# Transpositions alternate with the matmuls of the products on TensorE, and four engines get a new order of calls

## The chip, the cores and the metric

The kernel runs on one core of a Trainium2 chip. The metric is the time of the whole kernel on the device, in microseconds, as the median of the runs: 535.18 us before the change, over 3 runs (534.74 to 535.26).

A core has five engines that run side by side, each with its own list of instructions that it works through in order: TensorE (PE, matmuls and transpositions, results in PSUM), VectorE (DVE), ScalarE (ACT), GpSimd (POOL) and SyncE (SP, which only starts DMAs here). They meet only at semaphores.

## The reference

One decoder layer over x of shape (4, 1024, 256), with a context of (4, 77, 256). Cut to what is computed:

```python
# 1. self-attention with sigmoid weights, keys and queries normalised
q, k, v = x @ Wq.T + bq, x @ Wk.T + bk, x @ Wv.T + bv
attn = sigmoid(layer_norm(q) @ layer_norm(k).T / sqrt(256) - log(1024))
x = layernorm(x + ((attn @ v) @ Wo.T + bo) * layerscale)
# 2. cross-attention over 77 context rows, 16 heads of 16
a = softmax(qh @ kh.T / 4)
x = layernorm(x + (a @ vh) @ dense_w.T + dense_b)
# 3. feed-forward with a shift by one row
x_prev = x shifted down by one row
r = sigmoid((mu_r * x + (1 - mu_r) * x_prev) @ W_r.T)
k = (mu_k * x + (1 - mu_k) * x_prev) @ W_k.T
x = layernorm(x + r * (square(relu(k)) @ W_v.T))
```

## The kernel before

The 4096 rows of x are cut into 32 row tiles of 128 rows, t = 0 to 31, and 16 pairs of tiles (256 rows), i = 0 to 15, four pairs to a batch. The score work of self-attention is cut further, into 64 blocks, four to a pair.

**Products in three parts.** A product of two fp32 matrices is done as hi times hi, hi times lo and lo times hi, where hi is the operand rounded to fp32r and lo the rest. So every product is a run of 12 matmuls of 256 columns (6 of 512 columns for `qk`), all issued by `split_product` at line 298. ACT makes the hi part (line 477), DVE or POOL the lo part (line 1299, lines 971 and 990).

**Calls.** Each engine's program is a list of calls of small functions, one for each step and tile. On TensorE these are:
- products: `qk(t)` (queries and keys), `v(i)`, `scores(n)` and `attend(n)` (self-attention, n = 0 to 63), `query(i)` and `dense(i)` (cross-attention), `receptance(i)`, `mix_keys(i)`, `mix_values(i)` (feed-forward);
- transpositions of 128x128 fp32 blocks with the identity in `columns`: `tqk(t)` (line 1973, 4 turns), `x1(i)` and `x2(i)` (line 1885, 4 turns each), and `weights_t(t, c)` (line 2077), which turns the softmax weights of tile t in three groups c = 0, 1, 2 of 4, 4 and 2 turns. In all 576 turns;
- small fp32 matmuls: `cross_scores(t)` (line 2064, 32 rows at a time) and `mixed(i)` (line 2096, 32 columns at a time).

**Self-attention.** `scores(n)` fills one of two PSUM banks, ACT takes the sigmoid (`sigmoid`, line 553) and rounds it (`sigmoid_hi`), DVE makes the rest (`sigmoid_lo`), `attend(n)` multiplies with v and adds over the four blocks of a pair.

**Cross-attention of a tile.** `cross_scores(t)` fills four banks. DVE takes the largest of each head (`maxima(t, g)`, g = 0 to 3, line 1412), ACT takes 16 exponentials (`exponentials(t, g)`, four in a group, line 594), POOL adds halves (`fold_weights`, line 1047), DVE finishes sums and reciprocals, POOL multiplies (`normalise`, line 1052). Then `weights_t(t, c)` turns the weights into the first two of those banks, DVE copies them out (lines 1432 and 1438, ACT some), and `mixed(i)` and `dense(i)` follow for the pair. ACT has to load another table (line 545, helper `table_for`) whenever it changes between sigmoid and exponential.

Two waits matter below. `weights_t(t, 0)` writes into a bank of `cross_scores(t + 1)`, which has been issued before it, so it waits for the first group of that tile's exponentials; its second group of turns waits for the second:

```python
w.wait_ge(*pn_pool.at(t))            # normalise(t)
...
elif t + 1 < NT:
    w.wait_ge(*ex_act.at(t + 1, c + 1))
```

And `dense(i)` waits for the third group of exponentials of tile 2i+3, whose bank it writes.

**The order.** Each engine's list is written out by hand for the start and the end. Between them stand rounds: a function `round_(r)` holds the calls of one pair's worth of work on that engine, every stage some pairs behind the stage ahead of it, and `at(...)` leaves out the calls whose tile isn't there yet. The last 60 us or so are feed-forward work, with rounds `mix_round(i)` that place a few calls. No scheduler stands behind it: what is written is what the engine runs, in that order.

## Time and profile before

| | |
|---|---|
| median of the runs | 535.18 us (534.74 to 535.26) |
| span of the profiled execution | 531.8 us |
| PE busy | 515.0 us, 97% |
| PE weight loads | 468.3 us, 88% |
| ACT busy | 450.4 us, 85% |
| DVE busy | 443.7 us, 83% |
| POOL busy | 381.9 us, 72% |
| ACT table loads | 58, 74.4 us |

The span runs from the first to the last instruction of the one execution that the profiler recorded. It is 3.4 us shorter than the median of the timed runs, which have what lies around the instructions in them; the profile does not give the profiled execution's whole time apart. Sums are made against the span, and their difference is added to the median.

How to read it: a PE record of a matmul reaches from its start to a modelled end, and the next one starts long before that, so "busy" does not say that TensorE runs at its peak. What a matmul costs is the distance from its start to the start of the next one. Where rows stand in order of time, the first column is the start and the second the duration; `x4` is four instructions merged into a row.

### The profile page before, as it was taken

To read this page: it belongs to the slowest core of one execution; us is meant where nothing else is said; L and a number is where in the kernel's file an instruction comes from. 1 tells how busy PE (TensorE), PEld (TensorE's weight loads), DVE (VectorE), ACT (ScalarE), POOL (GpSimd) and SP (SyncE) were. 2 spreads that over 40 slices of the span, in tenths; PEclk is the share of its full clock that TensorE was granted. 3 is DMA by queue.
4 is the path that set the end of the run, shared out by engine and by line. 5 is a ranking of instruction groups with operands and counts; after the bars stand their busy time and mean duration, and the time that the engine had idled before them with its cause. 6 is when DMAs were issued, how large, how long until landed. Compare 5 with 4: busy or idle time off the path is not lost.

```text
span 531.8 us, 12709 instructions
## 1 busy us (share of the span) xinstructions
PE 515.0 (97%) x4530; PEld 468.3 (88%) x4530; DVE 443.7 (83%) x995; ACT 450.4 (85%) x1130; POOL 381.9 (72%) x554
## 2 busy tenths in 40 slices
PE   9999999999999999999999999999999898999994
PEld 6888999898989898989898989999898787899994
DVE  4787868878888879797979797778878888999996
ACT  3765579998989898989898989899999899898965
POOL 1774747676867676767667675767778889897996
PEclk9999999999999999999999999999999999999998
DMA  6410120110010110101010100020511000011122
GB/s 193 128 49 21 38 60 6 42 39 2 14 50 27 35 38 24 42 19 52 12 39 3 39 2 22 21 74 28 166 35 41 2 2 1 22 41 41 41 80 100
DMA packets 23269, 22.50 MB, mean 42 GB/s; under 512 B 1724, under 2 KB 23204, under 8 KB 23205
## 3 DMA queue, kind: packets, MB, share of 16 engines
q1 hardware_dynamic: 22770, 21.35, 12.7%
q8 instruction: 36, 0.59, 0.5%
q10 hardware_dynamic: 434, 0.34, 0.2%
q14 instruction: 29, 0.23, 0.2%
HBM read 14.55 MB, written 6.82 MB: 40 GB/s over the span
## 4 chain that ended last, share of the span: by engine, by line
PE 70%; ACT 12%; DVE 9%; issue 4%; POOL 4%; POOLq 0%; DVEq 0%; ACTq 0%
PE st L298 16%; PE acc L298 14%; PE xb L298 10%; PE proj L298 10%; PE xb L2077 5%; PE xb L2096 5%; ACT p_sb L594 4%; PE xb L2064 4%; DVE xm L1485 3%; ACT L545 2%; PE proj L1973 2%; PE xb L1885 1%; POOL rs L1110 1%; PE st L1893 1%; DVE kkT_lo L1299 1%
## 5 line engine op out<-in xcount | busy, mean ns | idle before, releaser
L594 ACT ACTIVATE p_sb<-xb,neg_mx 128x77 f32<-128x77 f32 x512 | 120.0, 366 | 5.2 <-DVE neg_mx L1412 4.9
L1047 POOL TENSOR_TENSOR fold<-p_sb 128x640 f32<-128x640 f32 x32 | 50.2, 1568 | 75.4 <-ACT p_sb L594 75.1
L1052 POOL TENSOR_TENSOR p_sb<-p_sb,rc 128x1280 f32<-128x1280 f32 x32 | 75.3, 2353 | 23.8 <-DVE rc L1425 23.7
L298 PE MATMUL acc<-vv_hi,aT_hi 128*128 128x256 f32 x256 | 76.6, 299 | 0.0
L545 ACT ACT_TABLE_LOAD x58 | 74.4, 1283 | 1.0
L298 PE MATMUL st<-qkT_hi 128*128 128x256 f32 x256 | 74.8, 292 | 0.0
L298 PE MATMUL st<-qkT_lo,qkT_hi 128*128 128x256 f32 x256 | 72.4, 283 | 0.0
L298 PE MATMUL st<-qkT_hi,qkT_lo 128*128 128x256 f32 x256 | 72.4, 283 | 0.0
L298 PE MATMUL acc<-vv_lo,aT_hi 128*128 128x256 f32 x256 | 72.2, 282 | 0.0
L298 PE MATMUL acc<-vv_hi,aT_lo 128*128 128x256 f32 x256 | 72.2, 282 | 0.0
L1412 DVE TENSOR_REDUCE neg_mx<-xb 128x4 f32<-128x308 f32 x128 | 53.7, 467 | 17.1 <-PE xb L2064 16.7
L553 ACT ACTIVATE a_sb<-st,nlogs 128x512 f32<-128x512 f32 x64 | 43.3, 679 | 16.4 <-PE st L298 16.3
L298 PEld LDWEIGHTS st<-qkT_hi 128*128 128x128 f32 x256 | 48.9, 191 | 4.9 <-issue 4.1
L1299 DVE TENSOR_TENSOR aT_lo<-a_sb,aT_hi 128x512 fp32r<-128x512 f32 x64 | 49.0, 767 | 4.1 <-ACT aT_hi L477 3.2
L298 PEld LDWEIGHTS acc<-vv_hi,aT_hi 128*128 128x128 f32 x256 | 48.6, 190 | 3.4 <-issue 3.3
L1432 DVE COPY pT<-xb 128x512 f32<-128x512 f32 x64 | 43.1, 676 | 10.1 <-PE xb L2077 9.8
L2077 PE MATMUL xb<-columns,p_sb 128*128 128x128 f32 x320 | 48.4, 274 | 1.7 <-DVE pT L1432 0.6
L298 PEld LDWEIGHTS st<-qkT_lo,qkT_hi 128*128 128x128 f32 x256 | 49.0, 191 | 0.2
L298 PEld LDWEIGHTS st<-qkT_hi,qkT_lo 128*128 128x128 f32 x256 | 48.9, 191 | 0.0
L298 PEld LDWEIGHTS acc<-vv_lo,aT_hi 128*128 128x128 f32 x256 | 48.8, 191 | 0.1
L298 PEld LDWEIGHTS acc<-vv_hi,aT_lo 128*128 128x128 f32 x256 | 48.7, 190 | 0.0
L477 ACT ACTIVATE aT_hi<-a_sb 128x512 fp32r<-128x512 f32 x64 | 43.2, 679 | 2.8 <-PE acc L298 2.6
(262 smaller groups left out, 1707.9 us busy)
## 6 DMA issues: line engine op xcount, KB each, us to landing
xs<-in_x SPq DMA_DIRECT2D x16, 256.0 KB, 3.0
xraw<-in_xT SPq DMA_DIRECT2D x15, 256.0 KB, 2.9
out_y<-y SPq DMA_DIRECT2D x15, 256.0 KB, 2.1
x_kept<-xs SPq DMA_DIRECT2D x10, 256.0 KB, 2.2
x2s_a<-x_kept SPq DMA_DIRECT2D x2, 512.0 KB, 5.0
x2s_b<-x_kept SPq DMA_DIRECT2D x2, 512.0 KB, 7.1
x2s_c<-x_kept SPq DMA_DIRECT2D x1, 512.0 KB, 3.7
cT<-in_cT SPq DMA_DIRECT2D x1, 308.0 KB, 3.3
```

What stands on the lines that cost most here:

```text
L298: mm = pe.matmul(out, s_, m_, start=first and k == 0 and q == 0, stop=last and k == n - 1 and q == 2, skip_group_check=not check)
L477: return act.activation(out, in_, ACT.Identity, **kw)
L545: act.activation(spare[:, n:n + 1], nlogs[:], func)
L553: act.activation(a_sb[:, i % NAR], st_bank[i % 2], ACT.Sigmoid, bias=nlogs[:, 0:1], scale=1.0 / 16).then_inc(sg_act.sem, 1)
L594: ex = act.activation(weights(t)[:, h // KH * (H // 2) + KH * n + h % KH, 0:SC], logits[n][:, h * SC:(h + 1) * SC], ACT.Exp, bias=neg_mx[: ...
L1047: pool.tensor_tensor(fold[:].rearrange("p (h k) -> p h k", k=FO), p[:, :, 0:FO], p[:, :, FO:2 * FO], ALU.add).then_inc(fo_pool.sem, 1)
L1052: pool.tensor_tensor(weights(t), weights(t), rc[:, t % 2].rearrange("p (h o) -> p h o", o=1) .to_broadcast([P, H, SP]), ALU.mult).then_inc ...
L1299: return dve.tensor_tensor(lo, whole, f(hi), ALU.subtract)
L1412: dve.tensor_reduce(neg_mx[:, t % 2, HG * n:HG * (n + 1)], logits[n][:, 0:HG * SC].rearrange("p (h k) -> p h k", k=SC), AX, ALU.min)\
L1432: dve.tensor_copy(pT[:, 4 * c:4 * c + 4, (t % 2) * P:(t % 2 + 1) * P], tiles(tp_bank(c), 4))\
L2077: mm = pe.transpose(tp_bank(c)[:, (n - 4 * c) * P:(n - 4 * c + 1) * P], p_sb[:, t % NP, n * P:(n + 1) * P], ident)
L2096: mm = pe.matmul(mixed_bank(i)[32 * n:32 * (n + 1), k * D:(k + 1) * D], vb[:, n, half, :, :, KC * b + k].rearrange("p a d -> p (a d)"), pT ...
```

## The change

On TensorE the four functions of transpositions (`tqk`, `x1`, `x2`, `weights_t`) become generators that give up control after each turn. `split_product` takes such a generator as `beside` and pulls one turn from it after each of its matmuls. `woven(product, i, turns...)` issues a product with turns between its matmuls, and what is left of the turns behind it; `alone(turns)` issues turns by themselves. The semaphore of a product or of a group of turns is still counted up by its own last matmul. About 550 of the 576 turns now stand between two matmuls of products; `weights_t(22, 2)`, `x2(0)`, `weights_t(31, ...)`, `x2(5)` and `x2(6)` stand alone.

```diff
+        NONE = iter(())
+
-        def split_product(pe, out, stationary, moving, first=True, last=True, check=True):
+        def split_product(pe, out, stationary, moving, first=True, last=True, check=True, then=None, beside=NONE):
             n = len(stationary)
             for k in range(n):
                 (sh, sl), (mh, ml) = stationary[k], moving[k]
                 for q, (s_, m_) in enumerate(((sh, mh), (sh, ml), (sl, mh))):
                     mm = pe.matmul(out, s_, m_, start=first and k == 0 and q == 0,
                                    stop=last and k == n - 1 and q == 2, skip_group_check=not check)
-            return mm
+                    if then and k == n - 1 and q == 2:
+                        mm.then_inc(then, 1)
+                    next(beside, None)
...
+        def alone(turns):
+            for _ in turns:
+                pass
+
+        def woven(call, i, *turns):
+            beside = chain(*turns)
+            call(i, beside)
+            alone(beside)
```

The second part is a new order of the calls on TensorE, ACT, DVE and POOL; the set of calls, the functions' waits, the buffers and the numbers that split work between engines stay as they are, and each engine issues as many instructions of each kind as before. The new round of TensorE is below whole. It runs for r = 7 to 12; what comes before and behind is written out.

```diff
                 def round_(r):
-                    at(attend, 4 * r - 18, NS, 9)
...
+                    attend(4 * r - 17)
+                    woven(qk, 2 * r, weights_t(2 * r - 13, 2))
+                    mixed(r - 7)
+                    scores(4 * r - 13)
+                    cross_scores(2 * r - 11)
+                    v(r)
+                    attend(4 * r - 16)
+                    attend(4 * r - 15)
+                    woven(dense, r - 7, weights_t(2 * r - 12, 0), tqk(2 * r))
+                    woven(scores, 4 * r - 12, x1(r - 5))
+                    qk(2 * r + 1)
+                    woven(query, r - 5, weights_t(2 * r - 12, 1), weights_t(2 * r - 12, 2))
+                    scores(4 * r - 11)
+                    cross_scores(2 * r - 10)
+                    scores(4 * r - 10)
+                    woven(attend, 4 * r - 14, weights_t(2 * r - 11, 0), tqk(2 * r + 1), weights_t(2 * r - 11, 1))
```

At the start, `on_all_rows(0)` and `on_all_rows(1)` (biases spread over all rows, line 1899) move ahead of `first_qk`, and `wvo()` comes before `qk(4)`:

```diff
                 warm_up()
+                on_all_rows(0)
+                on_all_rows(1)
                 first_qk()
-                on_all_rows(0)
                 qk(2)
                 qk(3)
-                on_all_rows(1)
-                qk(4)
-                tqk(0)
                 wvo()
+                woven(qk, 4, tqk(0))
```

In the written-out end of TensorE's list, `receptance(0)` to `receptance(2)` and `mix_keys(2)` move ahead of `cross_scores(31)`, `mixed(14)` is followed at once by `dense(14)`, and the three groups of `weights_t(31, ...)` stand in a row.

What stands in a row on TensorE in a round, before: the end of `dense`, and behind it the turns of the softmax weights, of queries and keys and of x, then the first matmul of `attend`.

```order
L298 MATMUL xb<-wx_lo,oT_hi 128x256
L298 MATMUL xb<-wx_hi,oT_lo 128x256
L2077 MATMUL xb<-columns,p_sb 128x128 [waits s_pn_pool]
L2077 MATMUL xb<-columns,p_sb 128x128 x3
L1973 MATMUL proj<-columns,qk_sb 128x128 [waits s_v_dve,s_qn_dve]
L1973 MATMUL proj<-columns,qk_sb 128x128 x3
L1885 MATMUL xb<-columns,xs 128x128 [waits s_ex_act,s_ln1_act]
L1885 MATMUL xb<-columns,xs 128x128 x3
L298 MATMUL acc<-vv_hi,aT_hi 128x256 [waits s_ln1a_dve,s_st_dve]
```

The same place after: the whole of `dense` with the turns of the weights and of queries and keys between its matmuls (the matmuls of products are at line 301 now, the turns at 2392 and 2286).

```order
L301 MATMUL xb<-wx_hi,oT_hi 128x256 [waits s_ex_act]
L2392 MATMUL xb<-columns,p_sb 128x128 [waits s_pn_pool]
L301 MATMUL xb<-wx_lo,oT_hi 128x256
L2392 MATMUL xb<-columns,p_sb 128x128
L301 MATMUL xb<-wx_hi,oT_lo 128x256
L2392 MATMUL xb<-columns,p_sb 128x128
L301 MATMUL xb<-wx_hi,oT_hi 128x256
L2392 MATMUL xb<-columns,p_sb 128x128
L301 MATMUL xb<-wx_lo,oT_hi 128x256
L2286 MATMUL proj<-columns,qk_sb 128x128 [waits s_v_dve,s_qn_dve]
L301 MATMUL xb<-wx_hi,oT_lo 128x256
L2286 MATMUL proj<-columns,qk_sb 128x128
```

The run of 12 turns is gone; each turn has a matmul of a product on either side.

The second place is the stretch behind `cross_scores` of an even tile, TensorE, before: `cross_scores`, then `attend` and `scores` (24 matmuls, of which the first and the last stand here), then the turns that wait for the exponentials of that tile.

```order
L2064 MATMUL xb<-kb,xq 128x154 x7
L298 MATMUL acc<-vv_hi,aT_hi 128x256 [waits s_st_dve]
...
L298 MATMUL st<-qkT_hi,qkT_lo 128x256
L2077 MATMUL xb<-columns,p_sb 128x128 [waits s_ex_act,s_pn_pool]
L2077 MATMUL xb<-columns,p_sb 128x128 x3
```

After:

```order
L2378 MATMUL xb<-kb,xq 128x154 x7
L301 MATMUL st<-qkT_hi 128x256 [waits s_sg_act]
...
L301 MATMUL st<-qkT_hi,qkT_lo 128x256
L301 MATMUL acc<-vv_hi,aT_hi 128x256 [waits s_v_pool,s_st_dve]
L2392 MATMUL xb<-columns,p_sb 128x128 [waits s_ex_act,s_pn_pool]
L301 MATMUL acc<-vv_lo,aT_hi 128x256
```

Between `cross_scores` and the first turn that waits for its exponentials there stand 13 matmuls now, where there were 24.

## Rows read from the trace of the kernel before

**Rows 1.** The page: busy time, share of the span and instructions of each engine.

```profile
PE 515.0 (97%) x4530; PEld 468.3 (88%) x4530; DVE 443.7 (83%) x995; ACT 450.4 (85%) x1130; POOL 381.9 (72%) x554
```

**Rows 2.** Busy by stretch: start:end, length; engines with counts, PEclk, DMA share, GB/s.

```profile
90.00:181.00 91.00, 90.88 (x829) 83.22 (x832) 77.39 (x168) 84.07 (x217) 60.89 (x77) 1.00 0.10 31
181.00:337.00 156.00, 156.00 (x1460) 143.39 (x1455) 132.84 (x295) 141.97 (x371) 106.89 (x146) 1.00 0.09 27
...
401.00:465.00 64.00, 58.50 (x569) 51.37 (x562) 56.51 (x134) 55.82 (x157) 57.02 (x71) 1.00 0.04 14
465.00:525.00 60.00, 58.17 (x473) 56.39 (x471) 57.11 (x141) 51.06 (x107) 54.54 (x101) 1.00 0.15 50
```

**Rows 3.** PE in order of time around groups of twelve and of two turns.

```profile
202.13 0.28 PE L298 MATMUL st<-qkT_hi,qkT_lo 128*128 128x256 f32 x1
202.25 0.60 PE L2077 MATMUL xb<-columns,p_sb 128*128 128x128 f32 x4
202.68 0.60 PE L1973 MATMUL proj<-columns,qk_sb 128*128 128x128 f32 x4
203.12 0.60 PE L2077 MATMUL xb<-columns,p_sb 128*128 128x128 f32 x4
...
203.68 0.28 PE L298 MATMUL acc<-vv_lo,aT_hi 128*128 128x256 f32 x1
...
204.87 0.28 PE L298 MATMUL acc<-vv_hi,aT_lo 128*128 128x256 f32 x1
204.99 0.38 PE L2077 MATMUL xb<-columns,p_sb 128*128 128x128 f32 x2
...
205.44 0.40 PE L298 MATMUL proj<-wqk_lo,xT_hi 128*128 128x512 f32 x1
205.68 0.39 PE L298 MATMUL proj<-wqk_hi,xT_lo 128*128 128x512 f32 x1
```

**Rows 4.** Weight loads (PEld) in order of time, behind the last turn at 203.45 us.

```profile
203.45 0.19 PEld L298 LDWEIGHTS acc<-vv_hi,aT_hi 128*128 128x128 f32 x1
203.56 0.19 PEld L298 LDWEIGHTS acc<-vv_lo,aT_hi 128*128 128x128 f32 x1
```

**Rows 5.** The start of the program, PE in order of time.

```profile
5.13 1.16 PE L1906 MATMUL xb<-wqk_hi,xT_hi 128*128 128x512 f32 x2
...
8.53 1.12 PE L1899 MATMUL st<-brow,ones 1*128 1x512 f32 x2
...
20.48 0.39 PE L298 MATMUL xb<-wvo_hi,xT_hi 128*128 128x256 f32 x1
```

**Rows 6.** PE in order of time where `tqk(9)` waits.

```profile
56.31 0.66 PE L1973 MATMUL proj<-columns,qk_sb 128*128 128x128 f32 x4 [0.28 <-DVE qk_sb L1352]
```

**Rows 7.** Steady round: first matmul behind `cross_scores`; then ACT from `query` to the exponentials.

```profile
199.27 0.39 PE L298 MATMUL acc<-vv_hi,aT_hi 128*128 128x256 f32 x1
...
197.38 0.84 ACT L477 ACTIVATE xq<-xb,columns 128x256 f32<-128x256 f32 x2
198.09 0.65 ACT L477 ACTIVATE aT_hi<-a_sb 128x512 fp32r<-128x512 f32 x1
198.76 1.28 ACT L545 ACT_TABLE_LOAD   x1
...
200.16 1.82 ACT L594 ACTIVATE p_sb<-xb,neg_mx 128x77 f32<-128x77 f32 x8
```

**Rows 8.** PE near 353 us, where 12 matmuls lie between `cross_scores` and the turns.

```profile
351.63 0.39 PE L298 MATMUL acc<-vv_hi,aT_hi 128*128 128x256 f32 x1
...
353.46 0.63 PE L2077 MATMUL xb<-columns,p_sb 128*128 128x128 f32 x4
```

**Rows 9.** PE in order of time: two late waits.

```profile
423.72 0.81 PE L2064 MATMUL xb<-kb,xq 32*128 32x154 f32 x16 [1.54 <-DVE oT_lo L1299]
...
434.07 0.81 PE L2064 MATMUL xb<-kb,xq 32*128 32x154 f32 x16 [0.72 <-ACT xq L477]
```

**Rows 10.** DVE in order of time, behind the last copy of turned weights.

```profile
455.73 0.68 DVE L1299 TENSOR_TENSOR kkT_lo<-st,kkT_hi 128x512 fp32r<-128x512 f32 x1
```

More of the change, by code:

```diff
@@ new lines, in _ @@
+                for r in range(7, 13):
+                    round_(r)
+                attend(35)
+                woven(qk, 26, weights_t(13, 2))
+                mixed(6)
+                scores(39)
+                cross_scores(15)
+                v(13)
+                attend(36)
+                attend(37)
+                woven(dense, 6, weights_t(14, 0), tqk(26))
+                woven(scores, 40, x1(8))
+                qk(27)
+                woven(query, 8, weights_t(14, 1), weights_t(14, 2))
@@ new lines, in _ @@
+                woven(qk, 29, x1(9), weights_t(16, 2))
+                scores(45)
+                query(9)
+                attend(42)
+                cross_scores(18)
+                attend(43)
+                woven(scores, 46, weights_t(17, 0), tqk(29), weights_t(17, 1), weights_t(17, 2))
+                mixed(8)
+                qk(30)
+                scores(47)
+                cross_scores(19)
+                v(15)
+                scores(48)
+                scores(49)
+                attend(44)
```

1482 lines of the change are left out of this document (854 added, 628 removed).

## The prediction

> **What bounds the kernel now.** I read the page's busy times first, then the busy time by stretch, then TensorE's instructions in order of time, and last what the others do where TensorE waits. The reader should see this in them. TensorE is busy 97% of the span [rows 1], and in the two steady stretches it has 90.88 of 91.00 and 156.00 of 156.00 us at the full granted clock (PEclk 1.00) [rows 2]. There the next matmul starts as soon as the one before lets it, so the time of this half of the kernel is a sum of distances between TensorE's starts, and an order can't shorten it unless it makes a distance shorter. ACT has 84.07 of 91 and 141.97 of 156 us there (92 and 91%), with no room for a much faster TensorE. From 401 us on it is another kernel: TensorE has 58.50 of 64.00 us, then 58.17 of 60.00, and DVE has 57.11 of those last 60 [rows 2]. So TensorE's rate counts to about 400 us, chains of waits from there, and at the very end DVE's queue too. I use the span of 531.8 us for sums, and add their difference to the median of 535.18.
>
> **A turn between two matmuls.** What does a turn cost now? In the run of twelve, the last matmul ahead starts at 202.13 and the second one behind at 203.68 [rows 3]: 1.55 us for twelve turns and two matmuls of 256 columns. Such matmuls follow each other after 0.12 (202.13 to 202.25 is one). That leaves 1.31 us, 0.109 a turn. In the group of two, 204.87 to 205.44 is 0.57 us; less 0.12 for the first matmul and 0.23 for the 512-column one behind (205.44 to 205.68 is 0.24) it is 0.22, or 0.11 a turn. This is the number that decides the change. Every group has one step from a matmul to a turn and one from a turn to a matmul, and in a group of two these weigh six times as much per turn as in a group of twelve. If the steps were cheaper or dearer than turn after turn, the two figures would differ. They don't, to about 0.005 a turn. Alternating makes everything out of these two steps, so a pair of matmul and turn costs 0.12 + 0.109 = 0.229 us, as it does in groups. The weight loads say why the step back is no shorter: the load for the matmul behind the last turn (203.45) begins with that turn and the next one at 203.56, 0.11 later, when that matmul has taken the array [rows 4]. [...]
>
> For some 550 turns that move, the ends are: +0.01 us each if the steps cost what the rounding of the rows leaves open, +5 us in all; and below, the rival of a cheap turn. I take 0, since both groups give it.
>
> The Trainium skill has another number here: "TensorE: Matmul & The Clock Gate", Back-to-back issue gap, gives N / 2.4 + 2.5 ns between matmuls at full clock, which is 56 ns for 128 columns. The same page lets the next load run under the matmul in flight. By that rule a turn between two matmuls, its load hidden, would cost 0.056 and the change would save 0.053 us on each turn; the rows above show 0.11 even for a turn whose load has a matmul to hide under, so this is a rival and not the forecast.
>
> **The start.** `on_all_rows` moves ahead of `first_qk`. Now `first_qk` begins at 5.13, with its first matmuls slow, and ends by 8.53, where the first `on_all_rows` starts [rows 5]; each takes some 1.05 us. Moved, these 2.1 us run while x and the weights are still landing and being rounded, so `first_qk` starts near 7.2 to 7.6 and finds what it needs. `wvo` then needs `fold_wo` on POOL, done by about 11 in the new order, before TensorE gets there at 13. By 20.48, where `v(0)` starts now [rows 5], I find four waits of 0.15 to 0.3 us that lose their place. Together 1.0 us less, between 0 and 1.5. What covers it: the rounding of x on ACT moves behind `qk_biases`, by about 1.5 us; if that isn't covered by the 1.4 us of TensorE's first half of `first_qk`, the gain is gone.
>
> **17 to 90 us.** TensorE waits here for nine short moments, 2.6 us together, the longest for `tqk(9)`, 0.44 us late at 56.31 [rows 6]. In the new order most of them have more matmuls ahead: `tqk(8)` to `qk(9)` has 2.4 us of TensorE's work between, where 1.4 stood in the case that waited. `tqk(9)` itself keeps its 4.4 us behind `qk(9)`, and so its wait. I take 1.5 us less, between 0 and 2.5.
>
> **The steady rounds.** A round has the same calls, so the same 25.9 us. What changes is how near the calls stand to what they wait for. One got too near. `weights_t(2r-11, 0)` waits for the first four exponentials of tile 2r-10. In the round shown, the first matmul behind `cross_scores` starts at 199.27 and the exponentials at 200.16; eight take 1.82, so the fourth is done at about 201.2 [rows 7]. ACT comes to them straight from `query`: 0.84, 0.65 for a rounding, 1.28 for the table, and the new order has the same row of calls. So the turn can start 1.9 to 2.0 us after that matmul. It has 24 matmuls ahead of it now, 2.9 us and no wait. After, it has 13: 13 x 0.12 and the slow first one, 1.65. TensorE then stands for 0.3 us. There is a place in the trace of before where only 12 are ahead: the turns start at 353.46, 1.83 after the matmul at 351.63, where 1.54 would do, 0.29 late [rows 8]. Nothing hides this, since TensorE has no slack. The close distance comes for odd tiles 3 to 19, nine times: +2.7 us, between 0 (if ACT comes earlier) and 4.5. The other waits of a round have something left by the same count: `dense` 0.35 us, `mixed` 0.3, `query` 0.7.
>
> **340 to 465 us.** TensorE loses about 9 us in waits. The new order mends some: tiles 21, 23, 24, 26 and 27 have the turns spread over a product, where two or three groups in a row each waited up to 0.3, -1.0; `dense(13)` comes later behind the exponentials, -0.6; `query(15)` has more ahead, -0.35. It makes others: `dense(14)` directly behind `mixed(14)` has to wait for ACT and DVE to split that result, and the same wait, with nothing between, is 1.54 us at 423.72 [rows 9], +1.5; `cross_scores(24)` and `cross_scores(30)` stand nearly behind their `query`, where the wait was 0.72 with one group of two turns between [rows 9], +1.2; three groups of `weights_t(31)` in a row, then `x2(5)`, which needs all their copies, +1.0. Sum +1.75, between -3 and +5.
>
> **The last 60 us.** Products of the feed-forward part moved ahead of `cross_scores(31)`, and DVE's calls with them. Behind its last copy of turned weights DVE has one `key_squares_lo` (0.68 us [rows 10]), two `gated` and one statistics call less to do, 3.1 us, and DVE is 95% busy there. TensorE gets no shorter, and it has 1.8 us of idle time: I take -1.5, between -3 and +2 (`mix_keys(15)` now stands 6.7 us of TensorE's work behind `x2(15)`, where 14.4 were, and a chain of eight ACT and DVE instructions lies between).
>
> **The sum.** 0 - 1.0 - 1.5 + 2.7 + 1.75 - 1.5 = +0.45 us: a span of 532.25, a median of 535.6. This kernel's measurement can tell about 0.2%, 1.07 us, from no change. It is small terms of both signs that cancel, so its own range is wide: 532.5 to 539.
>
> **Rivals.**
> *A turn between matmuls is cheap.* If a turn's 0.109 is only the price of following another turn, by not having its load hidden, an alternated one could fall to half a 256-column matmul, 0.06. That is 0.049 x 550 = 27 us of TensorE. ACT stops it: at 92% busy it leaves 8% of the 247 us from 90 to 337, 20 us, and the turns there (some 300) give 15; beyond 400 us little arrives. About 520. Against it: turns that follow a matmul cost the same [rows 3]. Chance 0.05.
> *The order is better than I count.* If ACT reaches the exponentials of even tiles early enough, the 2.7 us go, and if more of the late 9 us and of DVE's 3 arrive, 3 to 4 us come off: about 531.5. For it: ACT and DVE lose work at the end and TensorE has products ready to fill waits. Chance 0.28.
> *The round is too tight.* If the 0.3 us on the turn also eats what `dense` and `mixed` have left (0.3 each), ACT's chain from `mixed` over the table load and the exponentials to the next `mixed` becomes the bound of the round. It decides once ACT's chain takes over 0.3 us more than I add up. Then each of some ten rounds takes 0.7 rather than 0.3 longer, and the late waits keep their +1.75: 535.2 + 7 - 2.5 - 1.5 + 1.75, about 540. For it: ACT at 92%. Against: nothing waits now. Chance 0.30.
> *It doesn't alternate.* The order of instructions shows matmul and turn in alternation; no chance of its own.
>
> **How the numbers follow.** Forecast 0.37, of which 0.28 within 0.2% and 0.09 above; cheap turn 0.05; better order 0.28; tight round 0.30. So faster 0.33, same 0.28, slower 0.39. The range of 8 in 10 leaves out the cheap turn and the outer part of the two others: 530.5 to 541. Cases of both signs hold most of it; the likeliest one's own range is 532.5 to 539.
>
> **What would show it.** A pair of matmul and turn 0.229 us apart from the next pair: right; 0.18 or less: the cheap turn. A steady round of 26.2 us rather than 25.9, with a wait of 0.3 on L2392 once a round: right; 25.9: the better order; 26.5 or more with waits at `mixed` or `dense`: the tight one. The start of `v(0)`'s first matmul at 19.0 to 19.5, not 20.48. A wait of 1.5 us on `dense(14)`. I would be wrong if turns in alternation had another price, or if waits of over 1 us arose in a round on `scores` or `attend`, for which I counted distances of ten matmuls and more.

## The result: 50 us slower, far outside the range

The changed kernel takes 585.42 us (median of 4 runs, 583.66 to 586.12), the kernel before, on the same chip, 535.22 us (534.74 to 535.88). The ratio is 1.0933, 95% interval [1.0913, 1.0952]. The forecast was 535.6 us, its range 530.5 to 541.0.

The page of after and its busy time by stretch, to be read beside [rows 1] and [rows 2] (the columns are the same):

```profile
span 584.1 us, 12714 instructions
...
PE 530.6 (91%) x4530; PEld 480.6 (82%) x4530; DVE 494.3 (85%) x995; ACT 453.5 (78%) x1130; POOL 400.6 (69%) x554
...
PEclk9999999999999998989998999989999999999997
```

```profile
90.00:181.00 91.00, 84.46 (x757) 76.07 (x756) 81.97 (x150) 74.65 (x200) 56.41 (x71) 1.00 0.08 23
181.00:337.00 156.00, 144.18 (x1254) 130.80 (x1253) 135.29 (x256) 127.94 (x321) 102.28 (x126) 0.97 0.08 25
```

Two things stand out. TensorE, which had 90.88 of 91.00 and 156.00 of 156.00 us in [rows 2], now stands idle for 6.5 and 11.8 us there, and in the second stretch its granted clock is 0.97, no longer 1.00. And DVE is busy for 50.6 us more (494.3, not 443.7) with the very same 995 instructions, POOL for 18.7 us more with its 554. Instructions that nobody changed have become longer.

What TensorE waits for, from the view of waits of after (us in total, times, longest), the three largest. The view counts a wait from the modelled end of the matmul before, which lies 0.16 us and more behind the point where the next one could have started, so the time lost is larger than it says:

```profile
PE proj L2286 <- DVE qk_sb L1513: 20.9, 15, 2.0
PE xb L2392 <- ACT p_sb L610: 5.4, 9, 2.0
PE acc L301 <- DVE aT_lo L1460: 3.0, 3, 2.1
```

The first is the group of turns `tqk(2r+1)`, dealt into `attend(4r-14)`; it waits for `qk_norm` on DVE. In order of time on PE it looks like this:

```profile
220.85 0.30 PE L2392 MATMUL xb<-columns,p_sb 128*128 128x128 f32 x1 [0.31 <-ACT p_sb L610]
...
221.10 0.27 PE L2392 MATMUL xb<-columns,p_sb 128*128 128x128 f32 x1
...
223.93 0.33 PE L2286 MATMUL proj<-columns,qk_sb 128*128 128x128 f32 x1 [1.98 <-DVE qk_sb L1513]
...
225.49 0.41 PE L2392 MATMUL xb<-columns,p_sb 128*128 128x128 f32 x1
...
225.91 0.41 PE L2392 MATMUL xb<-columns,p_sb 128*128 128x128 f32 x1
```

The wait on the exponentials is 0.31 us in this view. From start to start it is 0.59 us (220.26, the matmul ahead of the rows shown, to 220.85) where 0.12 is usual, so 0.47 us are lost, for a forecast of 0.3. The stand of 1.98 us was not forecast, and behind it the pairs of matmul and turn lie 0.42 us apart (225.49 to 225.91) instead of 0.23: the clock is at its lower level, from 224.7 to 228.1. That happens five times before the last 8 us of the span.

Over the three rounds from tile 10 to tile 16 after takes 89.5 us and the kernel before 77.7. I added up how much longer each distance between two starts on TensorE is than the median of the same two kinds of instruction where nothing waits: of the 11.8 us, 6.4 lie ahead of turns of `tqk` that wait for `qk_norm`, 2.9 in the two stretches at the lower clock, and 1.4 on the exponentials.

Now DVE's forms of instruction (busy us, mean ns), first of the kernel before, then of after. They are the three whose mean changed by more than 0.1 us among those with over ten instructions:

```profile
L1299 DVE TENSOR_TENSOR aT_lo<-a_sb,aT_hi 128x512 fp32r<-128x512 f32 x64 | 49.0, 767 | 4.1 <-ACT aT_hi L477 3.2
L1350 DVE TENSOR_TENSOR qk_sb<-qk_sb,rs 128x512 f32<-128x512 f32 x26 | 19.1, 734 | 0.6 <-POOL nb L984 0.6
L1352 DVE TENSOR_TENSOR qk_sb<-qk_sb,nb 128x512 f32<-128x512 f32 x26 | 18.1, 698 | 0.9
```

```profile
L1460 DVE TENSOR_TENSOR aT_lo<-a_sb,aT_hi 128x512 fp32r<-128x512 f32 x64 | 67.7, 1060 | 1.6 <-ACT aT_hi L493 1.6
L1511 DVE TENSOR_TENSOR qk_sb<-qk_sb,rs 128x512 f32<-128x512 f32 x26 | 34.6, 1332 | 2.5 <-POOL nb L1090 2.4
L1513 DVE TENSOR_TENSOR qk_sb<-qk_sb,nb 128x512 f32<-128x512 f32 x26 | 28.9, 1110 | 0.9
```

These 116 instructions hold 45.0 of DVE's 50.6 us. They have in common that both their inputs lie in SBUF. Among those with over ten instructions, the ones with an input in PSUM, the statistics and the reductions kept their durations. The place where TensorE stands, in order of time on DVE and on POOL:

```profile
220.47 1.74 DVE L1511 TENSOR_TENSOR qk_sb<-qk_sb,rs 128x512 f32<-128x512 f32 x1
222.24 1.64 DVE L1513 TENSOR_TENSOR qk_sb<-qk_sb,nb 128x512 f32<-128x512 f32 x1
```

```profile
220.39 1.27 POOL L1101 TENSOR_TENSOR xs<-xs,bo 128x512 f32<-128x512 f32 x1
221.62 1.71 POOL L1077 TENSOR_TENSOR xT_lo<-xraw,xT_hi 128x512 fp32r<-128x512 f32 x1
223.29 1.72 POOL L1096 TENSOR_TENSOR vv_lo<-v_sb,vv_hi 128x512 fp32r<-128x512 f32 x1
```

In the new order of POOL, `residual1`, `xt_lo` and `v_lo` stand directly behind the odd `qk_deviation`, and so run exactly while DVE does the `qk_norm` that this `qk_deviation` released. I added up from the records how long POOL's instructions of over 1 us overlap DVE's three forms: 22.7 us in the kernel before, 82.9 in after. The normalisation of the weights overlapped them for 1.5 us and now for 19.4, the folding for 1.4 and 14.4, the three above for 6.8 and 35.9. The kernel before had its collisions too, but few, and 8.9 of its 22.7 us are beside an instruction of two columns that e8 below finds harmless.

### The profile page after: what moved, and what is told of

It reads as the page before. It is cut to its first block, busy times and chain, and to the rows that moved or that the text cites. A ratio compares the mean times of both kernels' runs of the same rounds, so it can differ in the third digit from the quotient of the medians.

```text
span 584.1 us, 12714 instructions
## 1 busy us (share of the span) xinstructions
PE 530.6 (91%) x4530; PEld 480.6 (82%) x4530; DVE 494.3 (85%) x995; ACT 453.5 (78%) x1130; POOL 400.6 (69%) x554
## 4 chain that ended last, share of the span: by engine, by line
PE 53%; DVE 20%; POOL 14%; issue 9%; ACT 4%; POOLq 0%; DVEq 0%; ACTq 0%
PE acc L301 11%; PE st L301 8%; PE xb L301 8%; PE proj L301 7%; PE xb L2392 5%; DVE qk_sb L1511 4%; PE xb L2413 4%; DVE qk_sb L1513 3%; DVE neg_mx L1573 3%; POOL p_sb L1158 2%; PE xb L2378 2%; PE proj L2286 2%; DVE aT_lo L1460 2%; POOL y L1228 1%; POOL y L1205 1%
## 5 line engine op out<-in xcount | busy, mean ns | idle before, releaser
L2392 PE MATMUL xb<-columns,p_sb 128*128 128x128 f32 x320 | 79.0, 281 | 7.5 <-ACT p_sb L610 5.4
L301 PE MATMUL acc<-vv_hi,aT_hi 128*128 128x256 f32 x256 | 80.2, 313 | 3.0 <-DVE aT_lo L1460 3.0
L301 PE MATMUL acc<-vv_lo,aT_hi 128*128 128x256 f32 x256 | 79.6, 311 | 0.0
L301 PE MATMUL acc<-vv_hi,aT_lo 128*128 128x256 f32 x256 | 79.2, 309 | 0.0
L301 PE MATMUL st<-qkT_hi 128*128 128x256 f32 x256 | 78.5, 307 | 0.0
L301 PE MATMUL st<-qkT_lo,qkT_hi 128*128 128x256 f32 x256 | 77.2, 301 | 0.0
L301 PE MATMUL st<-qkT_hi,qkT_lo 128*128 128x256 f32 x256 | 75.8, 296 | 0.0
L1460 DVE TENSOR_TENSOR aT_lo<-a_sb,aT_hi 128x512 fp32r<-128x512 f32 x64 | 67.7, 1060 | 1.6 <-ACT aT_hi L493 1.6
L2392 PEld LDWEIGHTS xb<-columns,p_sb 128*128 128x128 f32 x320 | 44.9, 142 | 10.5 <-issue 6.7
L301 PEld LDWEIGHTS acc<-vv_hi,aT_lo 128*128 128x128 f32 x256 | 51.2, 200 | 0.0
```

Source lines behind the costliest of these rows:

```text
L301: mm = pe.matmul(out, s_, m_, start=first and k == 0 and q == 0, stop=last and k == n - 1 and q == 2, skip_group_check=not check)
L1460: return dve.tensor_tensor(lo, whole, f(hi), ALU.subtract)
L2392: mm = pe.transpose(tp_bank(c)[:, (n - 4 * c) * P:(n - 4 * c + 1) * P], p_sb[:, t % NP, n * P:(n + 1) * P], ident)
```

## Theories, and a table for all experiments

**Theory P**: DVE's instructions with two inputs in SBUF and POOL's instructions that read SBUF hold each other up; the new order of ACT, DVE and POOL lays them side by side, TensorE waits for the stretched `qk_norm`, and its clock falls in these waits. Alternating has no part in it. **Theory T**: alternating itself costs the time on TensorE.

The table says where the time goes in each run: when ACT begins the exponentials of a tile (us from the start of the span), the distance from tile 10 to 12, which is a steady round, and the span.

| kernel | tile 0 | tile 1 | round | tile 19 | tile 31 | span |
|---|---|---|---|---|---|---|
| before | 74.70 | 83.36 | 25.91 | 316.06 | 442.36 | 531.8 |
| after | 76.15 | 89.72 | 30.35 | 355.79 | 493.45 | 584.1 |
| e1 before, alternating | 79.66 | 88.29 | 28.70 | 345.66 | 479.81 | 572.7 |
| e3 after, POOL fills | 72.90 | 83.12 | 26.41 | 321.92 | 451.36 | 541.4 |
| e4 after, norm fused | 72.88 | 84.46 | 28.01 | 335.71 | 472.55 | 562.2 |
| e6 before, POOL moved | 74.87 | 83.50 | 26.83 | 325.45 | 451.62 | 542.0 |
| e7 after, POOL moved | 76.35 | 89.71 | 27.04 | 342.08 | 479.70 | 569.9 |
| e10 as e3, groups ahead | 74.62 | 84.84 | 26.81 | 326.23 | 459.18 | 549.5 |

## Undoing the alternation, and doing it alone

**e1.** The kernel before with the alternation alone, its turns dealt into the product behind them:

```diff
+    for item in call:              # a product's matmuls
+        out.append(item)
+        if beside:                 # the turns that stood ahead of it
+            out.append(beside.pop(0))
+    out += beside
```

> The kernel before, with the alternation alone: each group of transpositions (576 in 89 groups) is dealt out between the matmuls of the product that stands directly behind it (527 groups now), and not one call changes its place on any engine. Every step of TensorE is recorded first and issued afterwards, so all its instructions have one line and are told apart by their tiles. Theory P (DVE's instructions with two inputs in SBUF are stretched by POOL, which the new order of ACT, DVE and POOL brings over them; alternating costs nothing): 533 to 541 us, DVE busy 440 to 448 us as in the kernel before, no clock under full after the start. Theory T (alternating itself costs the 50 us, on TensorE): 575 us or more.

574.69 us, ratio 1.0747 [1.0731, 1.0763]. Theory P, as I had put it, falls here: with nobody else's order touched and DVE at 443.6 us, alternating alone costs 40 us. But the price of a pair isn't what costs it. Between 90 and 340 us the median distance over matmul, turn and matmul is 0.231 us. What costs is seen in the view of waits of e1, between 90 and 340 us (from start to start the three rounds from tile 10 to 16 take 8.4 us more than before: 4.7 on the first of the two rows, 2.4 on the second, 0.8 on `cross_scores` waiting for `query`'s result):

```profile
PE proj L150 <- DVE qkT_lo L1383: 10.0, 17, 1.5
PE acc L150 <- DVE aT_lo L1383: 5.2, 9, 0.6
```

and on DVE in order of time:

```profile
249.66 0.69 DVE L1516 COPY pT<-xb 128x512 f32<-128x512 f32 x1 [1.28 <-PE xb L150]
250.27 0.68 DVE L1383 TENSOR_TENSOR aT_lo<-a_sb,aT_hi 128x512 fp32r<-128x512 f32 x1
251.21 0.69 DVE L1383 TENSOR_TENSOR qkT_lo<-proj,qkT_hi 128x512 fp32r<-128x512 f32 x1 [0.26 <-ACT qkT_hi L561]
```

DVE works off its list in order. Its copy of turned weights stands 1.28 us for the turns, which now end later, and everything behind it in the list, the rounding that `qk(2r)` needs among it, is late as well. I call that lateness: a result comes late and holds up what stands behind it in a list. e15 and e16 test it.

**e2 and e9.** The changed kernel with its order kept and only the alternation undone, the turns in a group behind their product (e2) or ahead of it (e9):

```diff
-            beside = chain(*turns)
-            call(i, beside)
-            alone(beside)
+            call(i)                    # e9: these two lines
+            alone(chain(*turns))       # the other way round
```

> The changed kernel with the alternation alone undone: the same calls in the same order on all engines, but the transpositions stand in a group behind the product that they were dealt into (576 in 93 groups). Theory P: 575 to 592 us, DVE busy near 490 us, the wait of 15 to 21 us on qk_norm before the transpositions of qk still there. Theory T: 530 to 545 us.

> The changed kernel with the alternation undone the other way: the same calls in the same order, with the transpositions in a group ahead of the product that they were dealt into. The groups end earlier than in the alternation and the products later by nothing (they end where they ended). The odd qk_norm is still late beside POOL. Theory P with latency: a group ahead of its product waits for qk_norm before 12 matmuls that could have run, so the wait grows by 0.5 to 1.5 us a round, while what waits for the turned result gains as much: 580 to 600 us. If alternation is only harmful in this order, by letting the turned results come late: 560 to 578 us.

594.64 us, ratio 1.1108 [1.108, 1.1137], and 592.52 us, 1.1076 [1.1046, 1.1106]: both slower than the changed kernel. DVE is busy for 496.3 and 491.5 us in them. So in the new order, undoing the alternation loses 7 to 9 us, and theory T falls as the account of the changed kernel: its 50 us are in the order. Both were foreseen by theory P (e2 a little above its range). In e9 the wait for `qk_norm` is the larger one, 24.9 us, as expected: a group ahead of its product meets it with nothing left to do.

**e15 and e16.** From e1, two turns in each gap (e15), and only the weights' turns alternating (e16).

> The kernel of the first experiment with two transpositions in each gap between matmuls instead of one. The last of twelve turns then ends after six matmuls instead of twelve, 0.7 us earlier. If lateness of the turned results costs the 40 us (waits of 0.6 us at qk and at attend in each half of a round): those waits shrink to 0 to 0.3 us each, 540 to 558 us. If each change between matmul and turn costs: half as many changes, so half of the 40 us, 555 us, but with the waits as before. If neither: 570 to 577 us.

> The kernel of the first experiment with only the transpositions of the weights (320 of 576) alternating; those of qk, x1 and x2 stand in a group ahead. If lateness costs: the wait of qk on the rounding of the turned qk (11.5 us in 20 places) is gone and with it a good part of the 40 us, 538 to 555 us. If alternating costs by its number: 320/576 of 40 us, 557 us, with no wait to show for it.

e15: 558.20 us, 1.0441 [1.0416, 1.0465]. Time alone fits both readings (half as many changes would give 555). The waits decide: the one on `qkT_lo` fell from 10.0 to 0.8 us between 90 and 340 us, which changes of instruction could not do. The one on `aT_lo` kept its 5.2 us, which I had expected to fall as well. e16: 582.73 us, 1.0894 [1.0871, 1.0917], and there I was wrong: fewer alternations, and yet more time. Its waits in the same stretch, first TensorE's, then those of DVE and ACT on TensorE:

```profile
PE proj L149 <- DVE qkT_lo L1384: 17.1, 16, 2.0
```

```profile
DVE pT L1517 <- PE xb L149: 31.5, 18, 2.8
```

```profile
ACT pT L562 <- PE xb L149: 33.1, 17, 4.0
```

I had left the turns of qk early, but their roundings stand in the lists of ACT and DVE behind copies of turned weights, and the weights' turns, starting later, hold up both lists (e1 has 22.6 and 5.6 us in these two rows). By number of alternations e16 should have been the cheaper. So it is lateness, and it works through the in-order lists: what counts is the latest turn that a list waits for. Not all of e16's 48 us is that: its granted clock fell five times before the end (2.2 us in the three rounds from tile 10 to 16), and DVE is busy for 453.0 us where e1 has 443.6.

## DVE beside POOL

**e3 and its control e5.** POOL as busy as before, but reading nothing in its large instructions; e3 in the changed kernel, e5 in the kernel before. In both the rounding of xT and v, the two residuals, the folding and the normalisation of the weights are not computed.

```diff
-                    pool.tensor_tensor(weights(t), weights(t), rc[:, t % 2]..., ALU.mult)
+                    write(p_sb[:, t % NP])                  # fill, and wait for it
+                    pool.memset(p_sb[:, t % NP], 0.5)       # fill again
```

> The changed kernel, in which POOL's six large kinds of instruction (rounding of xT and v, both residuals, the folding of the weights and their normalisation) are replaced by fills of the same tiles, two or three in a row, so that POOL is busy about as long (1.3, 1.6 and 2.3 us each) but reads nothing from SBUF in them. It leaves that computation out. Theory P, if it is POOL's reading that stretches DVE: the two instructions of qk_norm and the rounding of aT fall to 0.69 us each (from 1.33, 1.11 and 1.06), DVE busy 440 to 450 us, 535 to 552 us in all. If POOL's being busy at all stretches them: unchanged, 575 us or more. Theory T: 575 us or more, with DVE at 0.69 us.

> The kernel before with the same replacement on POOL as in the third experiment (six large kinds of instruction become fills of the same tiles that read nothing; their computation is left out). It is the control of that experiment: how much of its 41 us is only that POOL's work was replaced. Theory P: 531 to 537 us, since in the kernel before POOL's large reads lie beside DVE's instructions that don't mind them (aT_lo 0.77 us falls to 0.69, nothing on TensorE's path). If the replacement shortens chains by itself: under 528 us, and as much of the third experiment's gain was no gain of the reads.

e3: 543.49 us, 1.0166 [1.0145, 1.0187]; e5: 533.37 us, 0.9979 [0.9969, 0.9989]. DVE's forms in e3:

```profile
L1472 DVE TENSOR_TENSOR aT_lo<-a_sb,aT_hi 128x512 fp32r<-128x512 f32 x64 | 43.6, 684 | 2.2 <-ACT aT_hi L494 2.2
L1525 DVE TENSOR_TENSOR qk_sb<-qk_sb,nb 128x512 f32<-128x512 f32 x26 | 18.2, 698 | 0.9
L1523 DVE TENSOR_TENSOR qk_sb<-qk_sb,rs 128x512 f32<-128x512 f32 x26 | 18.1, 695 | 2.4 <-POOL nb L1103 2.2
```

POOL is busy for 375.0 us of 541.4 in e3, and the three forms are back at 0.69 us: it is POOL's reading, not its being busy. 41.9 us come back in the changed kernel, 1.5 to 1.9 in the kernel before, so about 40 of the 50 us hang on the collisions. In e3 the clock is 1.00 from 200 to 304 us, and a round takes 26.41 us.

**e8.** DVE beside POOL by itself, with no layer:

> No layer at all, but a measurement of DVE beside POOL: in ten phases DVE does five instructions of one kind in a row (two inputs in SBUF, one in PSUM and one in SBUF, TENSOR_SCALAR of 256 columns, copy of 512 columns, statistics of 256), alone, or while POOL does three TENSOR_TENSORs of 512 columns that read SBUF, four fills that only write, or seven on two columns; it writes zeros as the output. Theory P: with two inputs in SBUF 0.69 us alone and beside fills, 1.2 us or more beside reads; with one input in PSUM 0.68 us always; TENSOR_SCALAR 0.41 alone and over 0.6 beside reads; statistics 0.41 always; a copy from SBUF is open, 0.4 alone. If POOL's reads have nothing to do with it: the same durations alone and beside.

The forms, with mean ns behind the comma (a tile's name says what DVE does and what POOL does meanwhile). Each mean is over five instructions, of which the last one or two run alone, and of two_sbuf_reads the first too keeps 0.69 us; the numbers in the text are those of single instructions that run beside POOL:

```profile
L165 DVE TENSOR_TENSOR dve_two_sbuf_reads<-in_a,in_b 128x512 f32<-128x512 f32 x5 | 6.3, 1323 | 0.2 <-POOL pool_two_sbuf_reads L137 0.2
L173 DVE COPY dve_copy_reads<-in_a 128x512 f32<-128x512 f32 x5 | 4.9, 1052 | 0.2 <-POOL pool_copy_reads L137 0.2
L169 DVE TENSOR_SCALAR dve_scalar_reads<-in_a,col 128x256 f32<-128x256 f32 x5 | 4.5, 967 | 0.2 <-POOL pool_scalar_reads L137 0.2
...
L167 DVE TENSOR_TENSOR dve_psum_reads<-bank,in_b 128x512 f32<-128x512 f32 x5 | 3.1, 682 | 0.2 <-POOL pool_psum_reads L137 0.2
L173 DVE COPY dve_copy_alone<-in_a 128x512 f32<-128x512 f32 x5 | 1.8, 421 | 0.2 <-POOL pool_copy_alone L137 0.2
...
L171 DVE BATCH_NORM_STATS2 dve_stats_reads<-in_a 128x6 f32<-128x256 f32 x5 | 1.7, 417 | 2.6 <-POOL pool_stats_reads L137 2.6
L169 DVE TENSOR_SCALAR dve_scalar_alone<-in_a,col 128x256 f32<-128x256 f32 x5 | 1.7, 408 | 0.6 <-POOL pool_scalar_alone L137 0.6
```

With two inputs in SBUF it is 0.685 us alone and beside fills, and 1.75 us while POOL reads; POOL's own instruction goes from 1.27 to 1.71. Side by side, one of DVE's and one of POOL's start every 1.67 us, 0.16 us less than the sum of their distances alone (0.60 and 1.23): I read that as taking turns, one waiting for the other. So these engines meet at more than semaphores, which I had said was all. With an input in PSUM DVE keeps its 0.682 us, and the statistics keep theirs (0.417). The Trainium skill says this in "SBUF — State Buffer", Who interferes with whom: a VectorE instruction with two SBUF inputs contends with a GpSimd instruction that reads SBUF, not with one that only writes, and copies and TENSOR_SCALAR can contend by another mode. The runs agree (1.75 us beside reads, 0.685 beside fills; a copy 1.48 for 0.42, a TENSOR_SCALAR 1.35 for 0.41 beside reads). I had not weighed that rule when I predicted.

**e6.** The kernel before, with two of POOL's calls moved and nothing on TensorE:

```diff
                     at(qk_deviation, 2 * r + 5, NT, 12)
+                    at(residual1, r - 1, NJ, 3)
+                    at(xt_lo, r + 3, NJ, 7)
                     at(norm2, r - 6, NJ, 7)
```

> The kernel before with two of POOL's calls moved in every round and nothing else: the first residual and the rounding of xT (1.3 us each) stand directly behind the odd qk_deviation, so that they run beside qk_norm of the odd tile and the rounding of aT behind it; no matmul and no transposition changes place. Theory P: DVE's odd qk_norm goes from 0.7 to 1.2 to 1.7 us for one or both of its instructions, DVE busy 455 to 470 us instead of 444, and the time rises, 538 to 560 us. Theory T (it needs the alternation): 533 to 537 us. If DVE is stretched and TensorE does not notice, 533 to 537 us with DVE at 455 us or more.

543.89 us, 1.0171 [1.0155, 1.0186]. One of DVE's forms and the new largest wait of TensorE:

```profile
L1350 DVE TENSOR_TENSOR qk_sb<-qk_sb,rs 128x512 f32<-128x512 f32 x26 | 28.3, 1088 | 0.6 <-POOL nb L984 0.6
```

```profile
PE proj L1973 <- DVE qk_sb L1352: 7.3, 11, 1.2
```

The collision alone, with groups as they were, makes the wait and 9 us (543.89 for 534.88). This shows the cause from the other side.

**e7, e4 and e14.** Mends that compute everything. e7 moves `residual1` and `xt_lo` between the folding and the normalisation of the odd tile and `v_lo` behind the folding of the even one; e4 makes `qk_norm` one TENSOR_SCALAR per half; e14 does both.

```diff
-                    dve.tensor_tensor(both, both, scale, ALU.mult).then_inc(qn_dve.sem, 1)
-                    w.wait_ge(*qn_dve.at(i - NF, 1))
-                    dve.tensor_tensor(both, both, bias, ALU.add).then_inc(qn_dve.sem, 1)
+                    for m in range(2):
+                        half = qk_sb[:, i % 4, m * D:(m + 1) * D]
+                        dve.tensor_scalar(half, half, rs1[:, i % 4, m:m + 1], nb1[:, i % 4, m:m + 1],
+                                          ALU.mult, ALU.add).then_inc(qn_dve.sem, 1)
```

> The changed kernel with three of POOL's calls moved in every steady round: the first residual and the rounding of xT stand between the folding and the normalisation of the odd tile (POOL idles there for 3 us), the rounding of v behind the folding of the even tile. Beside the odd qk_norm POOL has nothing large left. Same result. Theory P: the odd qk_norm falls from 1.74 + 1.64 to 0.7 + 0.7 us in the six to seven rounds moved, TensorE's wait for it goes there and with it the half clock: 556 to 572 us. Theory T: 583 to 587 us.

> The changed kernel with qk_norm on DVE as one TENSOR_SCALAR for each half (256 columns, times scale plus bias from two columns of pointers) instead of two TENSOR_TENSORs of 512 columns with both inputs in SBUF. The same result. Theory P: two instructions of about 0.41 us in place of 1.33 + 1.11 us, whatever POOL does; TensorE's wait on qk_norm (20.9 us) goes, with the half clock behind it; the rounding of aT stays stretched: 548 to 565 us. Theory T: 575 us or more. If such an instruction is itself held up by POOL: over 0.6 us each and little gained.

> The changed kernel with both mends, POOL's three calls moved as in the seventh experiment and qk_norm as TENSOR_SCALARs as in the fourth. Same result. If the two take different collisions away: 585.4 less 13.8 less 21.0, 550 us, and not below, since the rounding of aT stays stretched beside the normalisation (theory P says 543 is out of reach without that). If they take the same ones away: 562 to 566 us. Theory T has no room for either.

e7: 571.64 us, 1.0685 [1.0667, 1.0703]; e4: 564.39 us, 1.057 [1.0527, 1.0612]; e14: 560.11 us, 1.0467 [1.0451, 1.0483]. The wait on `qk_norm` was 20.9 us and is 9.9, 9.7 and 3.3. In e7 both instructions of the odd `qk_norm` take 0.69 us again in the rounds moved, from 190 us on, where they took 1.74 and 1.64; the waits left lie ahead of that. In e4 I had expected 0.41 us whatever POOL does, and that was wrong. Its instruction takes 0.41 us alone and on average this:

```profile
L1511 DVE TENSOR_SCALAR qk_sb<-qk_sb,rs,nb 128x256 f32<-128x256 f32 x52 | 44.9, 903 | 2.5 <-POOL nb L1090 2.3
```

It collides as well, only with less to lose. e14 stays 17 us above e3; the rounding of aT is still at 1135 ns there, beside the normalisation. Its longest one, on DVE, and what POOL does meanwhile:

```profile
355.03 2.71 DVE L1461 TENSOR_TENSOR aT_lo<-a_sb,aT_hi 128x512 fp32r<-128x512 f32 x1
```

```profile
354.86 2.33 POOL L1158 TENSOR_TENSOR p_sb<-p_sb,rc 128x1280 f32<-128x1280 f32 x1 [0.80 <-DVE rc L1586]
```

DVE's ends 0.55 us behind POOL's, less than the 0.69 us that it takes alone: it stood for 2.0 of POOL's 2.33 us. TensorE stands 2.08 us for it, on `attend`. The two mends don't add up (14 and 21, together 25): they partly take the same collisions away, as the expectation's second case had it, though 560 lies just under that case's 562. No version here beats the kernel before.

## What alternating is worth, the clock, and the start

**e10.** e3's kernel with its turns in groups ahead, so without collisions; it leaves out what e3 leaves out.

> The third experiment's kernel (POOL's six large kinds as fills, their computation left out) with the transpositions in a group ahead of their product instead of alternating. Without the stretching of DVE this compares alternation and groups alone in the new order. If alternating costs and gives nothing by itself: 541 to 546 us, as the third experiment's 543.5. If alternation is what hides the waits of the turns on the exponentials and on qk_norm (0.3 us once a round seen there): 546 to 556 us. If it costs latency as in the first experiment: under 540 us.

550.25 us, 1.0283 [1.0258, 1.0308], 6.8 us more than e3. The wait on `qk_norm` is back with 3.3 us in 8 places, and the round takes 26.81 instead of 26.41. So in an order made for it, alternating hides waits of turns that are late, and is worth 7 us against groups ahead of their product (groups behind it weren't run without the collisions); in an order made for groups (e1) it costs 40. The price on TensorE is the same in both.

**e11 and e13.** Twelve thrown-away matmuls ahead of the wait of `tqk(13)`, `tqk(15)`, ... `tqk(31)`:

```diff
+                    if i >= 12 and i % 2:
+                        w.wait_ge(*tqk_dve.at(i - 1))
+                        for _ in range(12):
+                            pe.matmul(tqk_bank(i)[:, 0:D], w_qk[0][:, 0, 0:P], w_qk[0][:, 0, 0:D], start=True, stop=True)
                     w.wait_ge(*normed(i))
```

> The changed kernel with twelve matmuls of 256 columns more, of constants, into the bank that the odd transpositions of qk are about to write, ahead of their wait on qk_norm, for tiles 13 to 31: they fill 1.4 us of the 2 us for which TensorE stands there, and a product that is thrown away. Same result. If the half clock after such a stand costs what the trace says (five times 3.4 us at half clock, 1.7 us lost each): the clock stays full in the steady rounds and the time falls by 5 to 9 us, 576 to 581 us, though 0 to 0.5 us a round is paid where the wait was shorter than 1.4 us. If the clock costs nothing: 584 to 592 us.

> The kernel of the eleventh experiment once more, for a trace of an undisturbed execution. Twelve thrown-away matmuls stand in the wait of the odd transpositions of qk on qk_norm. By its times there (580.3 to 583.4 us) 2 to 5 us came back. If the half clock is what they save: no stretch of half clock behind those waits in the steady rounds (there were five in the changed kernel), and a round of matmul and transposition in pairs 0.23 us apart throughout. If not: half clock as before, and the time has another reason.

582.28 us, 1.0878 [1.0852, 1.0902], and again 581.95 us, 1.0882 [1.0855, 1.0909]: it is the same kernel twice, since the one execution of e11 that has a trace took 1795.61 us, for a reason that I didn't look for. The trace used is e13's. The same stretch in after and in e13 (columns as in [rows 2]):

```profile
200.00:380.00 180.00, 166.72 (x1495) 150.53 (x1494) 156.04 (x301) 148.04 (x375) 118.16 (x150) 0.97 0.09 27
```

```profile
200.00:380.00 180.00, 171.67 (x1570) 155.45 (x1562) 160.39 (x304) 149.97 (x384) 121.13 (x152) 1.00 0.09 26
```

In this stretch the clock stays full, and about 3 us come back (the intervals of the ratios just part: up to 1.0902 and 1.0909 against 1.0913 and more). I expected 5 to 9. By the distances between starts the five stretches at the lower clock cost after 7.4 us, some 1.5 each, and the two that e13 keeps (at 84 and 381 us) cost it 2.9. So the clock's part of the 50 us is small, and the saving is net of what the twelve matmuls cost where the wait was short.

**e12.** The kernel before with the start of the new order: `on_all_rows` ahead of `first_qk`, the biases ahead of the second half of x on ACT.

> The kernel before with the start of the new order alone: on_all_rows ahead of first_qk on TensorE, qk_biases and fold_biases ahead of the second half of x on ACT. Forecast of the prediction for this step: 1.0 us less, between 0 and 1.5: 533.4 to 534.9 us. If what the landing of x sets is the bound of the start: 534.5 to 535.5 us; if the biases now stand in front of the rounding of x on ACT, slower, up to 537 us.

535.99 us, 1.0024 [1.0007, 1.004]: slower by 1.1 us where I had forecast 1.0 less. Its single times lie between 533.9 and 537.9, wider than those of the kernel before (533.4 to 535.6). PE in order of time in e12, beside [rows 5], and then the same two groups of `first_qk` in the kernel before:

```profile
5.30 3.78 PE L1899 MATMUL st<-brow,ones 1*128 1x512 f32 x4
9.01 1.22 PE L1906 MATMUL xb<-wqk_hi,xT_hi 128*128 128x512 f32 x2
10.03 1.05 PE L1906 MATMUL xb<-wqk_hi,xT_lo 128*128 128x512 f32 x2
10.88 1.05 PE L1906 MATMUL xb<-wqk_lo,xT_hi 128*128 128x512 f32 x2
```

```profile
6.13 0.64 PE L1906 MATMUL xb<-wqk_hi,xT_lo 128*128 128x512 f32 x2
6.60 0.62 PE L1906 MATMUL xb<-wqk_lo,xT_hi 128*128 128x512 f32 x2
```

`first_qk` begins at 9.01 us, not at 5.13: its x and weights were there, but four matmuls of one row took 3.8 us ahead of it, and on ACT the biases stood ahead of the second half of x. Then two of its matmuls take 0.85 us from start to start where they took 0.47: TensorE runs at half the rate, and the record of a full clock begins at 13.0 us, not at 6.1. That goes with this start. Of the ten traces that have it (after, e12 and eight others), six get the full clock only at 13.0 to 13.6 us, and in the other four it falls once more, for 3.4 us, at 8.4 to 9.2; in all six traces with the old start it is full from 4.4 to 7.2 us on. `v(0)` begins at 20.57 to 23.01 us in the ten (22.33 in after, 22.90 in e12) and at 20.48 to 21.44 in the six. Whether the one-row matmuls do it was not tested by itself.

## Why the prediction was wrong, point by point

**What bounds the kernel** was right, and should have warned: with TensorE at 156.00 of 156.00 us, any wait that appears is paid in full.

**The turn between two matmuls** was right. Forecast 0.229 us for a pair, measured 0.231, so 0.111 a turn and not 0.109; the turn at half the price does not exist here. The reason given from the weight loads doesn't hold: in [rows 4] they last 0.19 us and begin 0.11 apart, so two are under way at once. And the 56 ns are, by the same section of the Trainium skill, the gap of a matmul by itself; for a stream in which each matmul has its weight load it has about 81 ns at 128 columns. Neither is a turn's price here.

**The start** had the wrong sign (e12, +1.1 us for -1.0). The failed step is that the 2.1 us of `on_all_rows` would run "while x and the weights are still landing": they took 3.8 us, `first_qk` began 3.9 us later, and it ran at half the rate. `v(0)` began at 22.33 us in after, where 19.0 to 19.5 was the sign of being right.

**17 to 90 us**: -2.5 us were forecast up to tile 1, the start included. e3, where nothing collides, shows -0.2, and after +6.4, with three waits on `qk_norm` of up to 1.9 us.

**The steady rounds**: this is the step that failed. The mechanism that I priced is there: the turn behind the exponentials, once a round, 0.47 us late in after and 0.17 in e3 (0.29 us from start to start where 0.12 is usual, too short for the view of waits). e3 has rounds of 26.41 us where I said 26.2. But "the other waits of a round have something left by the same count" was counted with the durations of the kernel before, for `dense`, `mixed` and `query` only. Neither `tqk` behind `qk_norm` nor what POOL does during `qk_norm` was in it. Each row of DVE was taken as a fixed length, and it is one only as long as POOL's reads lie elsewhere. From tile 1 to tile 19 the term was +2.7 us. It measures +6.1 without the collisions (e3: 238.8 for 232.7 us) and +33.4 with them.

**340 to 465 us**: tile 19 to tile 31 grew by 3.1 us in e3, inside the bounds given for +1.75; in after by 11.4. The wait of 1.5 us on `dense(14)` is there, with 1.4.

**The last 60 us**: from tile 31 on 89.5 us before, 90.0 in e3, 90.7 after. The 1.5 us less didn't arrive: DVE's lighter list was no gain.

**The rivals.** "The round is too tight" came nearest, and had the wrong engine and a sixth of the size: 0.7 us a round where 4.4 came, by ACT's chain where it was DVE's waiting for POOL. That all terms were small and cancelled was only so because the one large term was missing. Of the signs that I named as proof against me, waits of over 1 us in a round arose, on `tqk` and not on `scores`; `attend` has one of 2.07 us, at 382 us, behind the rounds, where a rounding of aT stands beside a normalisation as in e14's rows.

What stays open: without collisions (e3) 9.5 us of span remain, 6.1 between tiles 1 and 19, 3.1 from there to tile 31. Of them I can name 0.2 us a round on the exponentials; the rest was not tested by itself. And e3 removes every collision at once, so the 40 us aren't divided between `qk_norm`, the rounding of aT and POOL's own longer instructions.

## What to carry to other kernels

Before reordering, lay the lists of DVE and POOL side by side: a DVE duration taken from a trace holds only with the POOL neighbours that it had there. Moving three calls of POOL's gave back 14 us here (e7), with nothing else touched. A transposition costs the same wherever it stands, but its result has a place in somebody's in-order list; dealing turns between matmuls helps where they would have waited, and costs where a list waits for their copy. An experiment that keeps an engine busy but takes its reads away tells in one run what its reads do from what its being busy does.

## What the runs showed of the hardware

Where DVE and POOL take turns, both get longer: DVE's 0.69 us become 1.75 beside POOL's 1.27, which become 1.71. POOL's power of two columns (0.69 to 1.24 us each, also with inputs in SBUF) does next to nothing to DVE (0.68 to 0.73 us beside them), so the loss goes with how much POOL reads and not with how long it is busy. A TENSOR_SCALAR of 256 columns with one input in SBUF, 0.41 us alone, takes 1.35 us beside POOL's reads, so one input less is no protection; an input in PSUM is. And TensorE's granted clock went from 2.4 to 1.2 GHz, for 3.4 us each time, behind five of the eight stands of 1.94 to 2.07 us in after; behind a ninth, of 1.88 us at 573 us, it fell and stayed low to the end; behind the shorter ones there (up to 1.53 us) it never fell. The kernel before, whose longest stand was 1.54 us, kept its clock to the last 3.4 us.
